# Combine, norm and the attention's first norm in one stage, the state-space kernel's products beside the last experts, and no load stage

## The chip, the core and the metric

The kernel is one program for one core of a Trainium2 chip. The core has TensorE (matrix products, "PE"; its weight loads are "PEld"), VectorE ("DVE"), ScalarE ("ACT"), GpSimd ("POOL") and SyncE ("SP", which here only issues DMAs), 128-partition on-chip memory (SBUF), accumulators for products (PSUM, eight banks) and DMA queues. Each engine runs its own instruction list and meets the others at semaphores. The metric is the device time of one execution in microseconds, from the first to the last instruction and what lies around them.

## What is computed

Two decoder layers on 8 x 256 = 2048 tokens of width 256, all in float32 here. After each sub-layer f the state is x = layernorm(x + f(x)). The sub-layers in order: a state-space scan ("mamba"), cross attention, a mixture of 16 experts, a linear attention block ("performer"), a cross-attention with a state-space convolution, and a retrieval layer ("peer"). What the change touches, cut from the reference:

```
# mixture of experts: each token goes to its best expert, at most C = 160 tokens per expert
dispatch = einsum('tec,td->ecd', sec_mask, tokens)
h = relu(einsum('ecd,edh->ech', dispatch, w1)); expert_out = einsum('ech,ehd->ecd', h, w2)
ans = einsum('tec,ecd->td', combine_weights, expert_out)
# then x = layernorm(x + ans); and the performer starts with a norm of that
x1 = layer_norm(x, ln1_scale, ln1_bias)          # eps 1e-6
q, k, v = x1 @ wq, x1 @ wk, x1 @ wv
# state-space kernel of the later convolution: depends on weights alone
K = 2.0 * einsum('dn,dnl->dl', dC, powers).real;  Kf = rfft(K, n=2*L)
```

The kernel K has 256 taps for each of 256 channels. With tap = 16 h + l, it is, per channel d, a product of a table UU (128 x 16, over h) and a table VV (128 x 16, over l). The transform Kf is a product with a constant matrix ("dft_kernel").

## The kernel before

**Tiling.** The state X lies in SBUF as 16 tiles (NT) of 128 tokens x 256; XT is the same state transposed (2 blocks of 128 features x 2048 tokens). Norms work in groups of four tiles (GT). Every stage is a `Stage` with its own buffers, semaphores and a block: engines start it together and leave it together. Between the six big stages all semaphores are cleared and all engines meet (L2716 and around).

**Start.** `stage_load` (L135) asks for XT and ident and waits for both. `stage_mamba` (L514) then asks for W, WO and small weights on SP, in that order; TensorE waits for W (`w_loaded`) and makes, for each group of 512 tokens and each of four channel blocks, a product UP and a gate product ZP (L601). ScalarE (L609, L623) and VectorE (L633, L649 to 656) first wait for seven small loads (`loaded`). SP then loads X itself (2 MB) and, once TensorE's second products allow, stores rows (L572).

**Experts.** `moe_route` scatters the tokens to a buffer in DRAM; `moe_experts` (L1481) runs over 16 experts (numbered 0 to 15): TensorE turns the tokens, makes HP = tokens x W1 (L1560), later turns the last expert's answers back (L1543) and makes YT (L1573), which ScalarE copies (L1593); VectorE and ScalarE apply the relu (L1617, L1589); VectorE copies answers to YE (L1608) and SP stores them in DRAM (L1509). Beside this, GpSimd and ScalarE compute the tables UU and VV (`S4dTables`, L1117; the last step is L1253).

**Combine.** In a stage of its own, `norm_only` (L388) runs with `Combine` (L1256) beside it. TensorE makes 256 products of 16 x 16 outputs (L1299, one per channel); VectorE copies them eight times (L1315), each copy 512 columns wide on 16 partitions; SP moves the result within SBUF in 16 DMAs (L1292); TensorE transforms it (L1309) and VectorE copies it to KF (L1321). GpSimd gathers each token's answer from DRAM in 16 indirect DMAs (L1278). VectorE, behind its eight copies, adds the weighted answers (L1285) and norms X in place (L442 statistics, L445, L450 reciprocal, L408), one tile in four on GpSimd.

**Performer.** `stage_performer` (L1692) starts with a second `norm_only` (name pfln) that reads X, writes X1, and whose transposes (L480) ScalarE scales into XT (L501). Then a block in which GpSimd sets a buffer to one (L1722), and `products` (L166), the projections: 48 jobs on TensorE (L204) through a ring of eight banks, copied by VectorE alone (L1639, L1644, L1731).

What sets the order of work is this program order on each engine, and SP's and GpSimd's DMA queues, which take transfers in the order they are issued.

## Time and profile before

| | us |
|---|---|
| median of 3 timed runs | 2629.9 (2623.7 to 2634.0) |
| the profiled execution | 2615.5 |
| its span, first to last instruction | 2613.7 |
| TensorE busy in it | 2245.9 (86%) |
| VectorE busy | 1705.5 (65%) |
| ScalarE busy | 961.5 (37%) |
| GpSimd busy | 852.7 (33%) |

The profile is one execution; its times are to be compared with each other, and the span with the profiled execution's own time. Busy shares are means over stages with different limits, so a stretch is read in the timeline: each row gives start, duration, engine, line of the source, output and inputs by name, how many instructions were merged, and in brackets the engine's idle time ahead of it with what ended it.
### The profile page before, as it was taken

To read this page: it belongs to the slowest core of one execution; us is meant where nothing else is said; L and a number is where in the kernel's file an instruction comes from. 1 tells how busy PE (TensorE), PEld (TensorE's weight loads), DVE (VectorE), ACT (ScalarE), POOL (GpSimd) and SP (SyncE) were. 2 spreads that over 40 slices of the span, in tenths; PEclk is the share of its full clock that TensorE was granted. 3 is DMA by queue.
4 is the path that set the end of the run, shared out by engine and by line. 5 is a ranking of instruction groups with operands and counts; after the bars stand their busy time and mean duration, and the time that the engine had idled before them with its cause. 6 is when DMAs were issued, how large, how long until landed. Compare 5 with 4: busy or idle time off the path is not lost. (4 is left out here: it accounts for less than half of the span.)

```text
span 2613.7 us, 34978 instructions
## 1 busy us (share of the span) xinstructions
PE 2245.9 (86%) x12808; PEld 1537.1 (59%) x12808; DVE 1705.5 (65%) x4406; ACT 961.5 (37%) x1900; POOL 852.7 (33%) x471
## 2 busy tenths in 40 slices
PE   7788888998964994998995787879699889999997
PEld 2355555634654993465563444336466678888886
DVE  5799999515653126464147996541488788888886
ACT  2398898315846212055312432032123322222220
POOL 0198888004508954052011332431200111111110
PEclk9899999999987996999997888989799899999999
DMA  3121111000023662101000000020300000000001
GB/s 97 38 81 49 49 51 39 11 0 1 1 104 125 224 226 75 35 2 40 0 21 19 1 1 1 1 79 1 129 1 1 3 1 1 1 1 1 1 1 33
DMA packets 57902, 101.02 MB, mean 39 GB/s; under 512 B 7874, under 2 KB 39490, under 8 KB 56452
## 3 DMA queue, kind: packets, MB, share of 16 engines
q1 hardware_dynamic: 56196, 94.59, 10.8%
q0 software_dynamic: 1536, 4.20, 0.5%
q8 instruction: 102, 1.67, 0.3%
q14 instruction: 68, 0.56, 0.1%
HBM read 88.94 MB, written 9.57 MB: 38 GB/s over the span
## 5 line engine op out<-in xcount | busy, mean ns | idle before, releaser
L749 POOL TENSOR_TENSOR XT<-mamba_DU,scan_BS 128x1024 f32<-128x1024 f32 x128 | 299.1, 2361 | 156.3 <-DMA scan_BS<-mamba_rows 118.5
L878 DVE TENSOR_TENSOR_SCAN scan_H<-scan_AB,XT 128x512 f32<-128x512 f32 x256 | 296.2, 1208 | 8.5 <-POOL XT L749 5.0
L2488 PE MATMUL ex_HP<-XT,pe_DOWN 128*128 128x256 f32 x1024 | 246.5, 387 | 7.1 <-PEq L2334 6.3
L2519 PE MATMUL ex_OP<-pe_UP,ex_GH 128*128 128x256 f32 x1024 | 231.5, 380 | 0.0
L2549 ACT ACTIVATE ex_GH<-ex_HP 128x512 f32<-128x512 f32 x128 | 76.5, 599 | 379.3 <-PE ex_HP L2488 344.6
L763 PEld LDWEIGHTS scan_TP<-ident,scan_H 128*128 128x128 f32 x1024 | 120.1, 142 | 157.9 <-DVE scan_H L878 81.3
L808 ACT ACTIVATE scan_AB<-mamba_E,mamba_AA 128x510 f32<-128x510 f32 x256 | 198.7, 776 | 38.4 <-DVE scan_H L878 34.1
L2488 PEld LDWEIGHTS ex_HP<-XT,pe_DOWN 128*128 128x128 f32 x1024 | 192.0, 192 | 31.9 <-issue 6.4
L2519 PEld LDWEIGHTS ex_OP<-pe_UP,ex_GH 128*128 128x128 f32 x1024 | 194.0, 190 | 26.0
L772 PE MATMUL scan_YT<-mamba_BC,ident 128*128 128x512 f32 x384 | 198.5, 599 | 4.1 <-ACT scan_YS L824 2.3
L763 PE MATMUL scan_TP<-ident,scan_H 128*128 128x128 f32 x1024 | 147.6, 278 | 46.5 <-DVE scan_H L878 46.5
L2575 POOL TENSOR_TENSOR ex_AS<-ex_AS,pe_IV 128x512 f16<-128x512 f16 x32 | 52.9, 1683 | 361.9 <-DVE ex_AS L2623 361.9
L2600 DVE TENSOR_TENSOR ex_L<-ex_IOTA,ex_KEYS 128x4096 f16<-128x4096 f16 x64 | 151.8, 2372 | 2.2
L817 ACT ACTIVATE mamba_BC<-scan_TP,scan_CT 128x512 f32<-128x512 f32 x192 | 129.6, 675 | 3.9 <-PE scan_TP L763 3.9
L2346 PE MATMUL sides_QP<-XT,sides_WQ 128*128 128x512 f32 x256 | 118.1, 616 | 5.2 <-ACT sides_QN L2371 3.0
L2674 DVE SCALAR_TENSOR_TENSOR ex_GH<-ex_GP,ex_GH 128x1024 f32<-128x1024 f32 x64 | 78.4, 1224 | 61.1 <-issue 32.5
L1617 DVE TENSOR_SCALAR experts_HT<-experts_HP 128x320 f32<-128x320 f32 x32 | 15.7, 492 | 132.6 <-PE experts_HP L1560 132.6
L2036 PE MATMUL tk_TP<-tk_DG,tk_PP 128*128 128x128 f32 x256 | 55.2, 403 | 47.3 <-ACT tk_DG L2129 47.3
L2508 PEld LDWEIGHTS ex_GP<-ex_R,ex_L 128*128 128x128 f16 x2048 | 77.8, 117 | 17.3 <-DVE ex_L L2600 5.2
L2346 PEld LDWEIGHTS sides_QP<-XT,sides_WQ 128*128 128x128 f32 x256 | 49.0, 197 | 62.8 <-issue 55.8
L2508 PE MATMUL ex_GP<-ex_R,ex_L 128*128 128x32 f16 x2048 | 77.6, 191 | 9.2 <-issue 4.7
L2036 PEld LDWEIGHTS tk_TP<-tk_DG,tk_PP 128*128 128x128 f32 x256 | 52.0, 311 | 54.9 <-ACT tk_DG L2129 54.9
(417 smaller groups left out, 4639.5 us busy)
## 6 DMA issues: line engine op xcount, KB each, us to landing
moe_W<-in_L_ffn_w SPq DMA_DIRECT2D x32, 1024.0 KB, 7.5
scan_BS<-mamba_rows SPq DMA_DIRECT2D x64, 256.0 KB, 3.1
pe_DOWN<-in_L_ffn_down SPq DMA_DIRECT2D x1, 4096.0 KB, 13.4
pe_UP<-in_L_ffn_up SPq DMA_DIRECT2D x1, 4096.0 KB, 22.8
moe_dispatch<-s4t_BOTH SPq DMA_DIRECT2D x1, 2560.0 KB, 8.7
experts_XE<-moe_dispatch SPq DMA_DIRECT2D x16, 160.0 KB, 2.4
moe_answers<-experts_YE SPq DMA_DIRECT2D x16, 160.0 KB, 3.2
XT<-in_xT SPq DMA_DIRECT2D x1, 2048.0 KB, 7.4
```

The lines of the kernel that those rows point to most:

```text
L749: pool.tensor_tensor(BU[:, r % 2, cs], tokens(DU, cs, r // DS), row, ALU.mult).then_inc(bu_ready, 1)
L763: ins = pe.transpose(TP[:, i % SLOTS, c * P:(c + 1) * P], H[:, r % 2, c, tb * P:(tb + 1) * P], ident[:, 0:P])
L772: pe.matmul(YT[:, tb, :], ident[:, 0:P], HT[:, n % 4, :], start=(s == 0), stop=(s == DS - 1)).then_inc(y_added, 1)
L808: act.activation(later(AB[:, n % 2, :]), later(tokens(E, c, g)), ACT.Exp, scale=AA[:, 2 * c, s:s + 1], bias=AA[:, 2 * c, s:s + 1]).then_in ...
L817: act.activation(HT[:, n % 4, :], TP[:, item(r, tb) % SLOTS, :], ACT.Copy, scale=CT[:, TB * g + tb, s:s + 1]).then_inc(act_read, 1)
L878: v.tensor_tensor_scan(H[:, r % 2, c], AB[:, n % 2, :], BU[:, r % 2, c], 0.0, ALU.mult, ALU.add).then_inc(h_ready, 1)
L2036: ins = pe.matmul(TP[:, n % 2, 0, k * P:(k + 1) * P], PP[:, n % 2, h, k * P:(k + 1) * P], DG[:, h, :], start=(h == 0), stop=(h == XH - 1))
L2346: ins = pe.matmul(QP[:, g, :], WQ[:, k, c * P:(c + 1) * P], XT[:, k, g * G4:(g + 1) * G4], start=(k == 0), stop=(k == KD - 1))
L2488: ins = pe.matmul(HP[:, n % 2, a, :], DOWN[:, k, 2 * q + a, :], XT[:, k, b * BLK:(b + 1) * BLK], start=(k == 0), stop=(k == KD - 1))
L2508: ins = pe.matmul(GP[:, n % 2, t, :], L[:, n % 2, t // RUN, :, t % RUN], R[:, n % 2, t // RUN, :, t % RUN], start=True, stop=True)
L2519: ins = pe.matmul(OP[:, m % 2, 0:D], GH[:, b % 2, j, a * P:(a + 1) * P], UP[:, j, :], start=(j == 0), stop=(j == J2 - 1))
L2600: v.tensor_tensor(L[:, n % 2], numbers(P), along(0, P), ALU.is_equal).then_inc(left_ready, 1)
```

## The change

- `stage_load` is no longer run ahead of `stage_mamba`. There, SP issues W, the first 512-token group of XT, ident (in WO's place among the seven small loads), the small weights, the other three groups of XT, WO, X. TensorE waits for each group of XT, SP for WO.
- The state-space kernel's products move into `moe_experts`, in two chunks of 64 products, in experts 14 and 15 ahead of their YT products. One product takes two channels (32 x 32 outputs, of which the two 16 x 16 blocks on the diagonal are used) and goes to one of four 32-partition strips. VectorE copies a chunk at once (128 x 512) into KA, which reuses a table's buffer; SP stores the used blocks to a DRAM tensor in 2 x 8 DMAs, ahead of the last answers' store. The results YT lose their second PSUM buffer to the chunk.
- The stage with `Combine` and `norm_only` goes. `combine_norms`, the performer's first stage, gathers, adds, takes one set of statistics per tile, and from it gets both norms: X1 is normalised twice in one step on VectorE, X by ScalarE (128 x 256, scale and bias per token). GpSimd only gathers.
- The projections get four jobs more, at their end: the transform, with the kernel and its matrix loaded by SP during `combine_norms`.

The diff, cut (allocations of semaphores and small buffers, and the removed class `Combine`, whose code is that of the kernel before):

```diff
--- before.py
+++ after.py
...
+
+
+def first_group(io, XT, g):
+    tok = slice(g * G4, (g + 1) * G4)
+    return XT[:, :, tok], io["xT"].rearrange("(k p) t -> p k t", p=P)[:, :, tok]
...
                     @block.sync
                     def _(sp):
                         sp.dma_start(W[:], io["L0_attn_in_projT"].rearrange("(k p) n -> p k n", p=P)).then_inc(w_loaded, 16)
-                        sp.dma_start(WO[:], io["L0_attn_out_projT"].rearrange("(k p) n -> p k n", p=P)).then_inc(loaded, 16)
+                        sp.dma_start(*first_group(io, XT, 0)).then_inc(xt_loaded[0], 16)
+                        sp.dma_start(ident[:], io["ident"]).then_inc(loaded, 16)
...
+                        for g in range(1, NG):
+                            sp.dma_start(*first_group(io, XT, g)).then_inc(xt_loaded[g], 16)
+                        sp.dma_start(WO[:], io["L0_attn_out_projT"].rearrange("(k p) n -> p k n", p=P)).then_inc(wo_loaded, 16)
                         x_load.issue(sp)
                         x_load.wait(sp)
+                        sp.wait_ge(wo_loaded, 16)
...
                         for g in range(NG):
+                            pe.wait_ge(xt_loaded[g], 16)
...
-        pool.tensor_tensor(self.UU[:], self.UU[:], self.U2[:], ALU.add)
...
+        pool.tensor_tensor(self.UU[:], self.UU[:], self.U2[:], ALU.add).then_inc(self.factors_ready, 1)
...
+def moe_experts(nc, io, ident, dispatch, answers, kernel, tables, W1, W2, first_loads):
+    TILES = 4
+    PAIR = 2
+    KN = P // TILES
+    KI = KN // PAIR
+    CHUNKS = D // P
+    FIRST_CHUNK = NE - CHUNKS
     with Stage(nc, "experts") as st:
+        KA = tables.TT[:].rearrange("p d l -> p (d l)")[:, 0:CHUNKS * PAIR * LO * KI].rearrange("p (n a l i) -> p n a l i", n=CHUNKS, a=PAIR, l=LO)
         XE = st.sb("XE", [HC_, 2, 2, D])
...
-        YT = st.ps("YT", [P, 2, 512])
+        YT = st.ps("YT", [P, 512])
+        KP = st.ps("KP", [P, 512])
...
                 store(NE - 2)
+                for n in range(CHUNKS):
+                    sp.wait_ge(kernel_copied, n + 1)
+                    for j in range(TILES):
+                        for a in range(PAIR):
+                            r, d = j * KN + a * HI, n * P + j * KN + a * KI
+                            sp.dma_start(kernel[:, :, d:d + KI].rearrange("l h d -> h l d"), KA[r:r + HI, n, a]).then_inc(kernel_stored, 16)
                 store(NE - 1)
                 for i in range(2):
                     sp.wait_ge(stored[i], 16 * (NE // 2))
+                sp.wait_ge(kernel_stored, 16 * TILES * PAIR * CHUNKS)
 
...
+                def kernel_products(n):
+                    pe.wait_ge(tables.factors_ready, 1)
+                    if n:
+                        pe.wait_ge(kernel_copied, n)
+                    for i in range(KI):
+                        for j in range(TILES):
+                            d = slice(n * P + j * KN + i * PAIR, n * P + j * KN + (i + 1) * PAIR)
+                            ins = pe.matmul(KP[j * KN:(j + 1) * KN, i * PAIR * LO:(i + 1) * PAIR * LO], tables.UU[:, d, :].rearrange("p a h -> p (a h)"),
+                                            tables.VV[:, d, :].rearrange("p a l -> p (a l)"), start=True, stop=True)
+                    ins.then_inc(kernel_ready, 1)
...
                     if e:
                         turn_back(e - 1)
+                    if e >= FIRST_CHUNK:
+                        kernel_products(e - FIRST_CHUNK)
                     pe.wait_ge(relu_act, 2 * (e + 1))
                     pe.wait_ge(relu_dve, 2 * (e + 1))
-                    if e >= 2:
-                        pe.wait_ge(ys_copied, e - 1)
+                    if e:
+                        pe.wait_ge(ys_copied, e)
...
+                def kernel_out(n):
+                    v.wait_ge(kernel_ready, n + 1)
+                    v.tensor_scalar(KA[:, n].rearrange("p a l i -> p i a l"), KP[:].rearrange("p (i a l) -> p i a l", a=PAIR, l=LO), 2.0, None, ALU.mult).then_inc(kernel_copied, 1)
...
+def combine_norms(nc, name, X, X1, XT, ident, GA, rest, scale, bias, loads, ahead):
+    NG = NT // GT
+    with Stage(nc, name) as st:
+        TP = st.ps("TP", [P, 4, 512])
+        with st.block() as block:
+            @block.gpsimd
+            def _(pool):
+                for t in range(NT):
+                    pool.indirect_dma_start(out=GA[:, t, :], out_offset=None, in_=rest.answers,
+                                            in_offset=bass.IndirectOffsetOnAxis(ap=rest.FROM[:, t:t + 1], axis=0)).then_inc(gathered[t // GT], 16)
+            @block.sync
+            def _(sp):
+                loads.issue(sp)
+                for a in ahead:
+                    a.issue(sp)
+            @block.vector
+            def _(v):
+                ch = Chain(v, dve_chain)
+                for g in range(NG + 1):
+                    if g < NG:
+                        tiles = slice(g * GT, (g + 1) * GT)
+                        v.wait_ge(gathered[g], 16 * GT)
+                        for t in range(g * GT, (g + 1) * GT):
+                            ins = v.scalar_tensor_tensor(X[:, t, :], GA[:, t, :], rest.WT[:, t:t + 1], X[:, t, :], ALU.mult, ALU.add)
+                        ch.link(ins)
+                        for t in range(g * GT, (g + 1) * GT):
+                            ins = v.bn_stats(raw[:, t, :], X[:, t, :])
+                        ch.link(ins)
+                        for t in range(g * GT, (g + 1) * GT):
+                            ins = v.bn_aggr(MV[:, t, :], raw[:, t, :])
+                        ch.link(ins)
+                        v.tensor_scalar(RS[:, 0, tiles], MV[:, tiles, 1], 1.0, 1e-5, ALU.mult, ALU.add)
+                        v.tensor_scalar(RS[:, 1, tiles], MV[:, tiles, 1], 1.0 + 1e-6, 1e-11, ALU.mult, ALU.add).then_inc(var_ready, 1)
+                    if g:
+                        tiles = slice((g - 1) * GT, g * GT)
+                        v.wait_ge(std_ready, g)
+                        v.reciprocal(RS[:, :, tiles], RS[:, :, tiles]).then_inc(scale_ready, 1)
+                        v.wait_ge(scale_ready, g)
+                        for t in range((g - 1) * GT, g * GT):
+                            v.tensor_scalar(X1[:, t, :], X[:, t, :], MV[:, t, 0:1], RS[:, 1, t:t + 1], ALU.subtract, ALU.mult).then_inc(normed, 1)
+                        v.scalar_tensor_tensor(NB[:, tiles], MV[:, tiles, 0], -1.0, RS[:, 0, tiles], ALU.mult, ALU.mult).then_inc(bias_ready, 1)
+            @block.tensor
+            def _(pe):
+                for t in range(NT):
+                    pe.wait_ge(normed, t + 1)
+                    if t >= 4:
+                        pe.wait_ge(turned_read, t - 3)
+                    for k in range(KD):
+                        ins = pe.transpose(TP[:, t % 4, k * P:(k + 1) * P], X1[:, t, k * P:(k + 1) * P], ident[:, 0:P])
+                    ins.then_inc(turned, 1)
+            @block.scalar
+            def _(act):
+                loads.wait(act)
+                for g in range(NG + 1):
+                    if g < NG:
+                        tiles = slice(g * GT, (g + 1) * GT)
+                        act.wait_ge(var_ready, g + 1)
+                        act.activation(RS[:, :, tiles], RS[:, :, tiles], ACT.Sqrt).then_inc(std_ready, 1)
+                    if g:
+                        for t in range((g - 1) * GT, g * GT):
+                            act.wait_ge(turned, t + 1)
+                            for k in range(KD):
+                                ins = act.activation(XT[:, k, t * P:(t + 1) * P], TP[:, t % 4, k * P:(k + 1) * P], ACT.Identity,
+                                                     scale=scale[:, k:k + 1], bias=bias[:, k:k + 1])
+                            ins.then_inc(turned_read, 1)
+                        act.wait_ge(bias_ready, g)
+                        for t in range((g - 1) * GT, g * GT):
+                            act.activation(X[:, t, :], X[:, t, :], ACT.Identity, scale=RS[:, 0, t:t + 1], bias=NB[:, t:t + 1])
...
+            WK_ = s1.sb("WK_", [P, LO // LB, NF, P])
+            KB = s1.sb("KB", [P, LO // LB, D])
...
+                     (MASK[:], io["causal"]), (KEPS[:], io["L1_attn_key_eps"]), (WK_[:], io["dft_kernel"])] +
+                     [(KB[l * HI:(l + 1) * HI], inputs.kernel[l::LB].rearrange("i h d -> h i d")) for l in range(LB)])
+            GA = QT[:].rearrange("p c t -> p (c t)")[:, 0:NT * D].rearrange("p (t d) -> p t d", d=D)
+            combine_norms(nc, "pfln1", X, X1, XT, ident, GA, inputs, scale=LN[:, 0, :], bias=LN[:, 1, :],
+                          loads=Loads(nc, "pfln1", [(LN[:], io["L1_attn_ln"])]), ahead=[loads])
+            inputs.free()
...
+            def by_channel(v, out, product):
+                return v.tensor_copy(out.rearrange("p (m i a) -> p m a i", i=LO, a=2), product.rearrange("p (m a i) -> p m a i", i=LO, a=2))
+
+            for q in range(NF):
+                jobs.append((KF[:, q, :], [(WK_[:, i, q, :], KB[:, i, :]) for i in range(LO // LB)], by_channel))
             products(nc, "pfproj", jobs, loads, dve_only=True, ahead=[mlp_loads], evictor_needs=[loads])
...
-        stage_load(nc, io, X, XT, ident, with_x=stage_mamba not in stages)
+        if stage_mamba not in stages:
+            stage_load(nc, io, X, XT, ident, with_x=True)
...
```

## Rows read from the trace of the kernel before

**Rows 1.** Timeline from 0 to 25 us: start, us, engine, line, form [idle before].

```profile
0.73 0.43 SPq L99 DMA_DIRECT2D XT<-in_xT  x1
...
9.28 0.38 SPq L559 DMA_DIRECT2D mamba_in_W<-in_L_attn_in_projT  x1
9.71 0.46 SPq L560 DMA_DIRECT2D mamba_WO<-in_L_attn_out_projT  x1
...
14.37 3.78 PE L601 MATMUL mamba_in_UP<-XT,mamba_in_W 128*128 128x512 f32 x4 [14.37 <-DMA mamba_in_W<-in_L_attn_in_projT]
...
18.64 0.31 ACT L609 ACTIVATE mamba_AA<-mamba_AA 128x128 f32<-128x128 f32 x1 [8.08 <-DMA mamba_AA<-in_L_attn_A_log]
...
20.95 0.60 ACT L623 ACTIVATE mamba_in_SIL<-mamba_in_ZP 128x512 f32<-128x512 f32 x1 [0.70 <-PE mamba_in_ZP L601]
```

**Rows 2.** DMA issues of the page: KB each, us from issue to landing.

```profile
mamba_WO<-in_L_attn_out_projT SPq DMA_DIRECT2D x1, 512.0 KB, 6.2
```

**Rows 3.** Timeline from 970 to 986 us: the last expert and the next stage.

```profile
973.91 0.49 DVE L1617 TENSOR_SCALAR experts_HT<-experts_HP 128x320 f32<-128x320 f32 x1 [5.91 <-PE experts_HP L1560]
...
976.68 4.58 PE L1573 MATMUL experts_YT<-experts_HT,moe_W 128*128 128x160 f32 x32 [0.20 <-issue]
...
982.46 0.69 DVE L1608 COPY experts_YE<-experts_YP 80x512 f32<-80x512 f32 x1 [5.25 <-PE experts_YP L1543]
985.60 0.36 SPq L99 DMA_DIRECT2D combine_WK<-in_dft_kernel  x1
```

**Rows 4.** Timeline of GpSimd from 945 to 965 us: the last table step.

```profile
950.92 8.88 POOL L1253 TENSOR_TENSOR s_UU<-s_UU,s4t_U 128x4096 f32<-128x4096 f32 x1
```

**Rows 5.** Timeline from 985 to 1024 us; then the tile GA (ns min/median/max).

```profile
991.02 3.35 PE L1299 MATMUL combine_KP<-s_VV,s_UU 128*16 128x16 f32 x128 [0.76 <-issue]
...
991.76 1.02 DVE L1315 TENSOR_SCALAR combine_KA<-combine_KP 16x512 f32<-16x512 f32 x1 [1.52 <-PE combine_KP L1299]
...
1006.35 1.06 POOL L1278 DMA_INDIRECT s_GA<-moe_answers,moe_FROM  x1 [0.30 <-issue]
...
1010.48 1.66 DVE L1285 SCALAR_TENSOR_TENSOR X<-s_GA,moe_WT,X 128x256 f32<-128x256 f32 x4
...
1014.09 1.22 DVE L408 TENSOR_SCALAR X<-X,moenorm_MV,moenorm_RS 128x256 f32<-128x256 f32 x3
...
1015.23 1.66 DVE L1285 SCALAR_TENSOR_TENSOR X<-s_GA,moe_WT,X 128x256 f32<-128x256 f32 x4
...
1021.33 1.40 DVE L1321 COPY KF<-combine_KP 128x256 f32<-128x256 f32 x4
...
L1278 POOL DMA_INDIRECT s_GA<-moe_answers,moe_FROM x16: 942/947/2108, 986.3 to 1006.4; - x16
...
DMA to landing us min/median/max: 2.7/3.0/4.0
```

**Rows 6.** DMA from 15.5 to 17 us; the output stores of the page.

```profile
DMA packets 2199, 0.27 MB, mean 177 GB/s; under 512 B 1927, under 2 KB 2199, under 8 KB 2199
...
out<-X SPq DMA_DIRECT2D x4, 512.0 KB, 2.9
```

**Rows 7.** Timeline from 1024 us; window 1045 to 1051 (busy, PEclk, DMA).

```profile
1024.38 0.37 SPq L99 DMA_DIRECT2D pf_LN<-in_L_attn_ln  x1
...
1035.59 5.78 ACT L501 ACTIVATE XT<-pfln_TP,pf_LN 128x128 f32<-128x128 f32 x16
...
1045.48 9.82 PE L204 MATMUL pfproj_ring<-XT,pg_WQ 128*128 128x512 f32 x16 [6.10 <-PEq L1719]
...
1045.00:1051.00 6.00, 5.52 (x7) 2.45 (x8) 0.69 (x1) 0.00 (x0) 0.15 (x1) 0.50 0.67 234
```

**Rows 8.** Grouped lines (busy us, mean ns, idle before); then one row of the timeline.

```profile
L1403 PE MATMUL route_LT<-XT,route_GW 128*32 128x512 f32 x16 | 3.6, 1061 | 4.7 <-DMA route_TI<-in_spill_rows 4.7
...
L1034 ACT ACTIVATE attn_PR<-attn_SC,attn_MX 128x256 f32<-128x256 f32 x128 | 58.8, 479 | 7.6 <-DVE attn_MX L1074 7.6
...
1103.20 13.98 PE L204 MATMUL pfproj_ring<-pg_WV,XT 128*128 128x256 f32 x64
```

More of the change, by code:

```diff
@@ L467, in _ @@
             def _(pe):
-                if beside:
-                    beside.kernel_products(pe)
-                    beside.transform(pe)
                 if XT is not None:
@@ L1335, in stage_moe @@
                                                   for W, n in ((W1, "L0_ffn_w1"), (W2, "L0_ffn_w2"))])
[L1336 to L1343 removed]
+        tables = S4dTables(st, st, io)
+        moe_route(nc, io, X, XT, ident, TO, rest.FROM, rest.WT, dispatch, first_loads, tables)
+        moe_experts(nc, io, ident, dispatch, rest.answers, rest.kernel, tables, W1, W2, first_loads)
+    return rest
 def moe_route(nc, io, X, XT, ident, TO, FROM, WT, dispatch, first_loads, tables):
```

114 lines of the change are left out of this document (32 added, 82 removed).

## The prediction, made before the changed kernel was run

> **What bounds the kernel now.** The program is a row of stages with a barrier after each, so the time is a sum over stages, and each touched stretch has its own limit. I read in this order: the timeline of the first 25 us, the experts' end, the stretch from the experts to the projections, then single tiles, DMA counts and grouped lines for prices.
>
> Start. XT (2 MB) and ident are loaded in a stage of their own; the weight W is asked for only at 9.28, and TensorE's first product runs at 14.37. The first gate product is whole 6.6 us later (20.95), and ScalarE and VectorE's loop, which sets the pace from there on, starts with it [rows 1].
>
> Experts. TensorE is the chain: 32 records of W2 products in 4.58 us, as many of W1 before them, and only 0.20 us idle, while VectorE waits 5.9 us for it [rows 3]. GpSimd's last table step ends at 950.92 + 8.88 = 959.8 [rows 4].
>
> Then 59.9 us (985.60 to 1045.48 [rows 3, 7]) hold three things in a row: the state-space kernel (256 small products, 8 copies, 16 moves, a transform) with the gathers in its shadow; the combine and the first norm; after a boundary, the attention's norm.
>
> **Part by part.** The profiled run took 2615.5 us (span 2613.7); the median of the timed runs is 2629.9, 14.4 above. I sum against the profiled run and shift by those 14.4.
>
> *A, the load stage goes.* W is now issued first (0.73, where XT was), then group 0 of XT (512 KB). The trace has this pair in size: W and WO, 1 MB and 512 KB in succession. WO landed at 9.71 + 6.2 = 15.9, 6.6 after W's issue [rows 1, 2]. So TensorE starts at 0.73 + 6.6 = 7.3, not 14.37: -7.0. Bounds: as late after W's issue as now (5.1) gives -8.5; as late as the old load stage ended (9.28) gives -5.1. Seven small loads must land before ScalarE's first step; it now ran 9.4 after W's issue (18.64), and there is one DMA more ahead of it: 10.6. ScalarE is ready for the gate 1.6 later (20.95 less its idle of 0.70, less 18.64 [rows 1]), 12.2; the gate product comes at 7.3 + 6.6 = 13.9. Hidden by 1.7 us. XT's groups 1 to 3, WO and x follow on SP: group 1 is needed only after four products of group 0, WO stages later, and the row stores behind SP's new wait for WO come after TensorE's first projections. Nothing.
>
> *B, the products in experts 14 and 15.* 256 products become 128, 64 in each of two chunks, two channels in one (32 by 32), written to four column strips. A product is two matmul records, so a chunk has 128 of them. 128 records of the 16-column form take 3.35 us, with the idle before them 4.1 [rows 5]. I take 3.6 a chunk and subtract the 0.2 idle: +7.0 on the chain; nothing on TensorE hides them. The other end: for the gate's logits four strips ran side by side, 16 records of 512 columns in 3.6 us, 0.23 each [rows 8], where lone ones take 0.94 (four in 3.78 [rows 1]). If that held for 32 columns a chunk would be 0.9 and the term +1.6. I take the dear end: 16 columns take 26 ns and 160 take 143 [rows 3], so the small ones are not paced by their columns, and strips need not help.
>
> The Trainium skill speaks on both sides. TensorEngine Tiling (Array Packing), Instruction Overhead: some 60 cycles per matmul however few its columns, an estimate of 25 ns; the 26 ns row agrees. TensorE: Matmul & The Clock Gate, Part 3, The mechanism: strips start about 4 ns apart. The second is a rival below.
>
> Waits and queues. The tables are ready 7 us before the first chunk. The results' PSUM buffer is single now, but the turn ahead already awaited its copy. VectorE's copy (16x512 took 1.02 us [rows 5]; for 128 partitions 0.7 to 1.1) falls in its idle of 5.9. On SP, 16 stores go in ahead of the last answers store, each of 256 runs of 64 B. Issues cost 0.38 to 0.46 in [rows 1]; for the finer ones I take 0.5: chunk 0 goes out from 981.3 to 985.3, chunk 1 to 989.3, and the last answers are copied at 983.15 + 7.0 = 990.2 [rows 3]. The last expert covers them with 0.9 to spare; that is gone at 0.55 each, and at 0.8 they cost 3 us. The data: reads of this grain ran at 2199 packets in 1.5 us on 16 engines, 11 ns each per engine [rows 6]; 4096 runs are then 3 us, hidden. No row has small runs written to DRAM. Lower bound 0; upper the output's store, 512 rows of 1 KB, 32 per engine, landing in 2.9 [rows 6]: 90 ns each, 256 per engine 23 us, which ends at 1004 instead of 992. I take +0.8, nearest to the reads. B together +7.8, from +1.6 to +20.
>
> *C, boundaries.* The boundary with the semaphores' clearing (1022.73 to 1024.38, 1.65 us [rows 5, 7]) moves to where a plain one stood, about 0.4: +1.25. The new stage starts at S = 985.6 + 7.8 + 1.25 = 994.7.
>
> *D, one stage for combine and both norms.* Gathers: first at S + 0.7, each 0.95 + 0.30, 3.0 to land [rows 5], so groups of four are there at S + 7.6, 12.6, 17.6, 22.6. VectorE per group: answers and statistics, 1010.48 to 1014.09 less a reciprocal of 0.18, plus two small steps, 3.75; later reciprocal, four normalisings (three took 1.14) and bias, 0.2 + 1.55 + 0.12 = 1.87 [rows 5]. With 0.2 lost to the 2.5 MB of loads that SP issues beside: group 1 from 12.8 to 16.55, then 0 to 18.4, group 2 to 22.15, 1 to 24.0, group 3 to 27.8, 2 to 29.65, 3 to 31.5. So from group 1 VectorE is the limit and the gathers have 1 us to spare. ScalarE: eight 128x128 at 0.37 a group, 2.95 (16 took 5.78 [rows 7]), and now four 128x256 with two pointers. No row shows these: 0.37 (half the columns) to 0.60; I take 0.45, near the exponential of this size at 0.48 [rows 8]. The tail is ScalarE's: group 2 from 29.1 to 32.1 and 33.9, group 3 to 36.9 and 38.7; I take S + 38.5. GpSimd's share of the normalising falls away; its cover is VectorE's 0.4 a group, counted above. The memset's block stays: 1041.37 to 1045.48, 4.1 [rows 7]. Projections start at S + 42.6, so C and D are 1.25 + 42.6 - 59.9 = -16.0; from -18 (gathers early, 0.37 on ScalarE) to -4 (every gather as slow as the one of 2.11). TensorE's clock is 0.50 at the projections' start [rows 7], and after a stretch with still less work on it it will be the same.
>
> *E, four transform jobs at the projections' end.* Each is four records of 128x256, as a value job: 64 such in 13.98 us [rows 8], 0.87 a job: +3.5. VectorE keeps up with a copy each; the tile's loads are long in place.
>
> Sum: -7.0 + 7.8 - 16.0 + 3.5 = -11.7. 2615.5 becomes 2603.8; by the median 2618.
>
> **Rivals.**
> *Forecast*, 3.5 us either way: 2614.5 to 2621.5.
> *Gathers exposed.* One of sixteen took 2.11 us [rows 5]. Should SP's loads do that to the first eight, the last lands 9.3 later; VectorE's lead takes part, and the stage ends some 5 us later: 2623; with all sixteen, 2630. Against: the last one took 1.06 beside the same VectorE work.
> *Strips side by side.* At 0.9 us a chunk the chain gains 5.4, but SP's stores then set the end, at about +4.5: 2614 to 2615. For it the logits row, against it the 26 ns. This is the second page's rule.
> *The small stores decide, slower than before.* Sixteen stores in one queue, the last answers and the stage's end behind them. They start at 981.3 and are free up to 990; each us more is one on the end, and the whole gain is gone when they take 20.5 us, 1.3 per store or 80 ns per run and engine. At 95 ns the result is 2633; one after another at a read's full landing of 3 us, 48 us and 2657. For it: no row has such writes. Against: 11 ns for such reads.
> *The load stage gives less*: -4 instead of -7 if a late small load holds ScalarE: 2621.
>
> **How the numbers follow.** Forecast 0.58, strips 0.16, gathers 0.12, small stores 0.08, load 0.06. The bound of 0.5% is 13.1 us (2616.8), about what a measurement of this kernel can tell from no change; the forecast lies on its edge, a third of it below. Faster 0.19 + 0.16 = 0.35; slower needs 2643, the far part of the stores and a little beside, 0.05; the rest, 0.60, is within. The range for 8 in 10 goes from strips with a cheap tail (2609) to exposed gathers (2629).
>
> **What would show it.** First product at 7.3. Experts 14 and 15 longer by 3.6 us each; the last answers store issued right behind VectorE's copy, the stage over some 2.4 us later. In the new stage VectorE without idle from group 1 on, ScalarE last. From the last W2 product's end to the projections 49 us, 64.2 now. Four jobs more, 3.5 us. Against it: SP still issuing when the last answers are copied, a store landing long after its issue, VectorE waiting for gathers, a chunk of 1 or 2 us. Only the price of 64-byte writes could make it wrong by far.

## The result, and the profile after

| us | before | after |
|---|---|---|
| median of 4 timed runs | 2632.0 (2623.7 to 2635.7) | 2598.4 (2593.4 to 2601.4) |
| the profiled execution | 2615.5 | 2596.8 |
| its span | 2613.7 | 2595.0 |

The ratio is 0.988, with a 95% interval of 0.987 to 0.990: some 31 us less by the ratio and 33.6 by the two medians, where 12 were forecast. 2598.4 lies below the range, which began at 2609. (The ratio and the medians differ by 2 to 3 us in several runs below; gains in us are differences of medians where nothing else is said.) The two profiled executions differ by only 18.7. That these numbers disagree is the key to the case.

The rows of after that answer to those of before come first. The timeline of its start and of its last two experts (start, us, engine, line, form, in brackets the idle before; answers to [rows 1, 3]):

```profile
7.72 3.75 PE L601 MATMUL mamba_in_UP<-XT,mamba_in_W 128*128 128x512 f32 x4 [7.72 <-DMA XT<-in_xT]
...
10.43 0.31 ACT L609 ACTIVATE mamba_AA<-mamba_AA 128x128 f32<-128x128 f32 x1 [8.41 <-DMA mamba_AA<-in_L_attn_A_log]
...
959.76 1.30 PE L1512 MATMUL experts_KP<-moe_VV,moe_UU 128*32 128x32 f32 x128
...
961.09 1.03 DVE L1584 TENSOR_SCALAR moe_TT<-experts_KP 128x512 f32<-128x512 f32 x1 [0.47 <-PE experts_KP L1512]
...
971.57 9.31 SPq L1478 DMA_DIRECT2D s_kernel<-moe_TT  x16
...
977.41 0.69 DVE L1580 COPY experts_YE<-experts_YP 80x512 f32<-80x512 f32 x1 [4.67 <-PE experts_YP L1502]
980.93 0.45 SPq L1461 DMA_DIRECT2D moe_answers<-experts_YE  x1
984.36 0.36 SPq L99 DMA_DIRECT2D pf_LN<-in_L_attn_ln  x1
```

The 16 small stores by themselves (line L1478; ns of one, min/median/max):

```profile
L1478 SPq DMA_DIRECT2D s_kernel<-moe_TT x16: 447/450/1924, 971.6 to 980.4; - x16
```

The reader is to see three things. A chunk of products takes 1.30 us. The 16 small stores hold SyncE's queue for 9.31 us: 0.45 for the issue of one, 0.49 from one to the next, except for one of them, the second, which takes 1.92. So the last answers, copied at 977.41 + 0.69 = 978.10, are sent out only at 980.93, 2.8 late.

The timeline of the new combining stage, from its start at 984.36 to the projections (answers to [rows 5, 7]):

```profile
985.07 1.06 POOL L1699 DMA_INDIRECT pg_QT<-moe_answers,rest_FROM  x1 [33.22 <-POOLq L2800]
...
988.58 4.62 SPq L99 DMA_DIRECT2D pg_KB<-s_kernel  x8
988.95 0.95 POOL L1699 DMA_INDIRECT pg_QT<-moe_answers,rest_FROM  x1 [0.30 <-issue]
...
996.66 1.67 DVE L1716 SCALAR_TENSOR_TENSOR X<-pg_QT,rest_WT,X 128x256 f32<-128x256 f32 x4 [18.56 <-DMA pg_QT<-moe_answers,rest_FROM]
...
1021.27 2.91 ACT L1757 ACTIVATE XT<-pfln_TP,pf_LN 128x128 f32<-128x128 f32 x8
1024.01 2.12 ACT L1762 ACTIVATE X<-X,pfln_NB,pfln_RS 128x256 f32<-128x256 f32 x4
1026.38 3.51 POOL L1800 MEMSET pg_VA<- 128x4096 f32 x1 [21.37 <-ACTq L1797]
...
1030.23 4.61 PE L204 MATMUL pfproj_ring<-XT,pg_WQ 128*128 128x512 f32 x5 [9.97 <-PEq L1797]
```

The issue of the fourth gather runs from 988.95 to 989.90, and its group is first worked on at 996.66, 7.7 after that issue began and 12.3 after the stage's start. ScalarE ends the stage at 1026.13, 41.8 after it.

### The profile page after: what moved, and what is told of

Same layout as the page of the kernel before. It is cut to its first block and busy times, and to the rows that moved or that the text cites. A ratio compares the mean times of both kernels' runs of the same rounds, so it can differ in the third digit from the quotient of the medians.

```text
span 2595.0 us, 34415 instructions
## 1 busy us (share of the span) xinstructions
PE 2226.3 (86%) x12552; PEld 1522.9 (59%) x12552; DVE 1689.6 (65%) x4368; ACT 967.7 (37%) x1912; POOL 839.9 (32%) x463
## 5 line engine op out<-in xcount | busy, mean ns | idle before, releaser
L2119 PE MATMUL tk_TP<-tk_DG,tk_PP 128*128 128x128 f32 x256 | 48.8, 368 | 48.4 <-ACT tk_DG L2212 48.4
L1545 PE MATMUL experts_YT<-experts_HT,moe_W 128*128 128x160 f32 x512 | 76.9, 310 | 7.2 <-ACT experts_HT L1561 6.8
```

## The experiments

Two theories at the start. The first: the change's own steps are worth 30 us, and I mis-sized them. The rival: the profile of before shows an execution that isn't like the timed ones.

**The two kernels again, and the change in two halves.** `e3` has the new load order alone (part A); `e4` all the rest (B to E).

> The kernel before, unchanged, run as if it were a variant: it tells how far two profiles and two sets of timed runs of one kernel lie apart. The sum over the touched stretches gives -11.7 us, the two profiled spans differ by 18.7, the timed medians by 33. Theory 'clock': the part beyond the stretches is TensorE's granted clock at the starts of later, untouched stages, which falls out differently from run to run; then this profile's span differs from 2613.7 by 5 to 20 us, at the starts of stages, and the ratio to before is 1.000 within 0.3%. Theory 'change': the extra belongs to the change; then this span is again within 3 us of 2613.7.

> The changed kernel again, on the chip of the other runs of this call. Theory 'clock' (the extra is chance): ratio nearer to 0.9955 (-11.7 us) than to 0.988. Theory 'change' (the extra is carried by one of its parts): ratio 0.988 again, -30 us.

> Only the load stage is removed, as in the change; all else as before. The sum gives -6.6 us at the first product and -6.2 at the scan: ratio 0.9976. If this part carries the extra 19 us of the timed runs, ratio 0.990 to 0.991.

> The changed kernel with the old load stage back. The sum over its stretches gives -8.6 up to the projections' start and +3.5 for the transform's jobs, -5.2 at the attention's core: ratio 0.998. If this part carries the extra, ratio 0.990 to 0.991.

Beside a kernel before at 2631.2 (23 runs): e1 2626.1 (ratio 0.998, 0.997 to 0.9995), e2 2600.1 (0.988, 0.986 to 0.990), e3 2625.3 (0.998, 0.997 to 0.999), e4 2606.7 (0.991, 0.990 to 0.993). But e1 is the kernel before itself, and it lies 5 us below the other runs of the same kernel: differences of that size mean nothing here. e3 is only 0.8 below e1, so the medians don't show what A is worth; its trace does, the scan starts at 114.7 and in e1 at 121.4. e4 is 19 us below e1 where the sum had 5, so the surplus is in B to E. The profile of e1 took 2629.0 and not 2615.5, 13.5 more. One place alone holds more than that: from the experts' first product to the attention's norm it has 228.0 us, 210.3 in the profile that I had, which is 17.7 more; the other stages together are some 4 us shorter. So neither theory of e1 had it right: the profile of before is not like the others, and not by the clock at the start of later stages. The TensorE timeline of that place, in e1:

```profile
985.33 1.83 PE L1299 MATMUL combine_KP<-s_VV,s_UU 128*16 128x16 f32 x64 [3.22 <-PEq L1504]
987.33 0.32 PE L1299 MATMUL combine_KP<-s_VV,s_UU 128*16 128x16 f32 x6 [0.17 <-issue]
988.09 0.34 PE L1299 MATMUL combine_KP<-s_VV,s_UU 128*16 128x16 f32 x6 [0.43 <-issue]
988.84 0.29 PE L1299 MATMUL combine_KP<-s_VV,s_UU 128*16 128x16 f32 x4 [0.42 <-issue]
```

and two windows of it (busy us and records of PE, PEld, DVE, ACT, POOL, then PEclk, DMA share, GB/s):

```profile
985.30:1008.80 23.50, 6.84 (x122) 4.55 (x122) 1.00 (x1) 1.28 (x1) 15.26 (x16) 0.51 0.39 112
1008.80:1019.10 10.30, 10.22 (x391) 10.11 (x391) 6.16 (x7) 0.00 (x0) 0.00 (x0) 0.78 0.02 5
```

In the first 23.5 us TensorE gets through 122 of the 512 records (two to a product), 64 at a stretch and then 58 in bursts, waiting for nothing that the profile shows ("issue"). These are the microseconds in which GpSimd has its 16 gathers on the way (x16 under POOL). The issue of the last gather runs from 1004.88 to 1005.83. With the 3.0 from issue to landing of [rows 5] it lands near 1007.9, and from 1008.80 on TensorE runs 391 records with hardly a gap. In the profile of before the block of 128 in [rows 5] took 3.35 us, and the whole row of 512 took 16. e3 shows the bursts as well.

**Are the gathers the cause?** e5 is the kernel before, with GpSimd waiting for the last product:

```diff
     def gather(self, pool):
+        pool.wait_ge(self.k_ready, D // self.DB)
         for t in range(NT):
```

> The kernel before, with one edit: GpSimd issues its 16 gathers of the experts' answers only after TensorE has done the state-space kernel products of that stage, not beside them. Theory (beside the gathers TensorE is fed its small matmuls in bursts of 1 to 6 every 0.7 us): the 512 products run without gaps in about 16 us, 985.3 to about 1001; the first gathers land some 5 us after that, and the additions are at work near 1010 where the kernel before has them near 1020; 8 to 11 us shorter than the kernel before, ratio 0.996 to 0.997. Rival (the products run in bursts by themselves, whatever GpSimd does): they still take 23 us, the gathers come behind them, and the kernel is 7 to 8 us longer, ratio 1.003.

```profile
987.33 4.61 PE L1300 MATMUL combine_KP<-s_VV,s_UU 128*16 128x16 f32 x170 [3.24 <-PEq L1505]
...
992.58 9.21 PE L1300 MATMUL combine_KP<-s_VV,s_UU 128*16 128x16 f32 x342 [0.64 <-issue]
```

The timeline of e5, TensorE: 512 records in 14.5 us. The statistics behind the first additions start at 1010.5, in e1 at 1021.6. VectorE then waits for later gathers (from there to the attention's norm it takes 25.2 us and took 20.6), so that the stage is 8.4 us shorter than in e1, at the low end of the forecast. The whole took 2623.9, ratio 0.998 (0.997 to 0.999) to a kernel before at 2628.6: 4.7 us less, no more than e1 shows for no change at all. Products by themselves don't come in bursts. That it is the gathers beside them is not shown yet, for e5 ran on another chip than e1.

The next step held the gathers only until half of the products are done (`D // self.DB // 2`), as e12 and again as e16; e11 and e18 issue plain copies of the same size in place of the indirect gathers, so that the sums are of other rows (arguments left out, `...`):

```diff
-            pool.indirect_dma_start(out=self.GA[:, t, :], out_offset=None, in_=self.answers, in_offset=...)
+            pool.dma_start(self.GA[:, t, :], self.answers[t * P:(t + 1) * P])
```

> The kernel before, with GpSimd's gathers issued after half of the 512 products are done. Theory (TensorE is short of instructions only while gathers are being issued): the first 256 products run unbroken in about 8 us, to 993.5; then bursts of 1 to 6 until the last gather has landed, near 1016, and the rest at 26 ns each; the last product is done at 1017 to 1021. Rival (only the start of a stage is short of instructions, before its code has been fetched once): the last 256 run unbroken too, and the last product is done at 1001.

> The kernel before, with each of GpSimd's 16 indirect gathers of the stage replaced by a plain copy of 128 consecutive rows, same bytes, same queue; this leaves out the choice of rows by the routing, so the sums are of other rows. Theory A (it is the indirect form, its descriptors made from indices, that keeps TensorE short of instructions): the products run unbroken, 16 us for 512, and the additions start at 1005 to 1010 instead of 1020: 10 to 15 us shorter than the kernel before. Theory B (any transfers that GpSimd issues there do it): bursts as before, additions at 1020, no difference beyond the shorter issue.

Neither showed bursts: e12 2615.4 (one run), e11 2611.9 (ratio 0.999, 0.9985 to 1.0004). But the kernel before took 2614.1 beside them (2607.8 to 2616.8, 15 runs), 10 to 17 us less than elsewhere. The records number the chips: these runs were on chip 11, those told of so far on 12 and 15. On chip 11 e12, with the gathers issued from 991.02 on, beside the second half of the products, ran like this:

```profile
983.17 4.61 PE L1300 MATMUL combine_KP<-s_VV,s_UU 128*16 128x16 f32 x170 [3.24 <-PEq L1505]
988.43 3.35 PE L1300 MATMUL combine_KP<-s_VV,s_UU 128*16 128x16 f32 x128 [0.65 <-issue]
992.16 3.35 PE L1300 MATMUL combine_KP<-s_VV,s_UU 128*16 128x16 f32 x128 [0.38 <-issue]
995.89 2.30 PE L1300 MATMUL combine_KP<-s_VV,s_UU 128*16 128x16 f32 x86 [0.38 <-issue]
```

So my theory was incomplete: in some places the gathers starve TensorE and in another they don't. The same kernel, as e16, went to chip 12, with both kernels beside it.

> The kernel before once more, for one more execution of its combining stage. The chip that is drawn decides: where its runs lie at 2624 to 2635 us the 512 kernel products come in bursts of 1 to 6 and the additions start near 1021; where they lie at 2608 to 2617 us the products run in about 17 us in blocks of 128 and the additions start near 1004.

> The kernel before with GpSimd's gathers issued after half of the products, once more. Theory (TensorE is short of instructions only on the chips where the kernel before takes 2624 us and more, and only while gathers are issued): on such a chip the first 256 products run in about 8 us and the rest in bursts until the last gather has landed, near 1014, last product 1014 to 1020; on the other kind of chip all 512 run in 17 us. Rival (only the start of a stage is short of instructions): no bursts on either.

> The kernel after once more, to see what the change is worth on the chip that is drawn. Theory (17.7 us of the gain is the short supply of instructions, which the kernel after does not meet anywhere): on a chip where the kernel before takes 2608 to 2617 us, the kernel after takes 2596 to 2603, 12 to 18 us less, ratio 0.993 to 0.995; where it takes 2624 to 2635, 30 us less, ratio 0.988. Rival (the kernel after is faster by its own work alone): 30 us less on either.

e16 on chip 12, TensorE and GpSimd:

```profile
989.77 3.35 PE L1300 MATMUL combine_KP<-s_VV,s_UU 128*16 128x16 f32 x128 [0.66 <-issue]
993.50 0.63 PE L1300 MATMUL combine_KP<-s_VV,s_UU 128*16 128x16 f32 x19 [0.38 <-issue]
994.38 0.31 PE L1300 MATMUL combine_KP<-s_VV,s_UU 128*16 128x16 f32 x6 [0.25 <-issue]
...
1013.58 0.19 PE L1300 MATMUL combine_KP<-s_VV,s_UU 128*16 128x16 f32 x1 [1.16 <-issue]
1014.98 3.97 PE L1300 MATMUL combine_KP<-s_VV,s_UU 128*16 128x16 f32 x143 [1.21 <-issue]
...
992.36 1.06 POOL L1279 DMA_INDIRECT s_GA<-moe_answers,moe_FROM  x1 [33.41 <-PE combine_KP L1300]
...
1011.23 0.94 POOL L1279 DMA_INDIRECT s_GA<-moe_answers,moe_FROM  x1 [0.30 <-issue]
```

TensorE ran without long gaps until 994.1, 1.8 us after the first gather's issue began, and again from 1014.98, 2.8 us after the last one's issue ended (1012.17). On this chip, then, the bursts follow the gathers when these are moved. e13 repeats e1: 64 records, then bursts, then 391 from 1007.58. Chip 12 showed the bursts on two occasions, and chip 11, between them, did not; chip 11 was seen only once, so "chip" may stand for something else of that hour. The kernel before took 2624.3 on chip 12 this time and e14 2600.8, ratio 0.990 (0.987 to 0.993); I had said 30 us and 0.988, and 24 were measured, though the runs of before there spread from 2621.9 to 2635.1.

**What of the gathers does it?** e18 (plain copies, again on GpSimd's queue) and e19 (the same copies issued by SyncE ahead of WK).

> The kernel before with plain copies of 128 consecutive rows in place of GpSimd's 16 indirect gathers, once more; the sums are of other rows. It tells something only where the kernel before lies at 2622 us and more. Theory A (the indirect form does it): no bursts, 512 products in 17 us, 10 to 18 us shorter than the kernel before. Theory B (any transfer that GpSimd issues does it): bursts until the last copy has landed, near 997, since 16 issues take 8.6 us there and not 20; products done near 1007, 10 to 12 us shorter.

> The kernel before with the same 16 plain copies issued by SyncE, ahead of its load of WK, and none by GpSimd; the sums are of other rows. Theory (transfers of GpSimd's own queue keep TensorE short of instructions): the 512 products run in blocks of 128 in 17 us on every chip, additions start near 1004, 15 to 18 us shorter than the kernel before where that lies at 2622 us and more. Rival (busy DMA engines do it, whoever fills them): bursts as long as the copies run, some 8 us at 2.1 MB, products done near 1008.

Both were on chip 8, the kernel before at 2626.0 (2624.2 to 2635.2). e18:

```profile
985.77 4.70 PE L1298 MATMUL combine_KP<-s_VV,s_UU 128*16 128x16 f32 x170 [3.24 <-PEq L1503]
991.03 3.35 PE L1298 MATMUL combine_KP<-s_VV,s_UU 128*16 128x16 f32 x128 [0.57 <-issue]
...
986.21 8.62 POOL L1278 DMA_DIRECT2D s_GA<-moe_answers  x16 [25.97 <-POOLq L1503]
...
q0 software_dynamic: 768, 2.10, 27.0%
```

The last row is the DMA of 985.7 to 1009.7: the same 768 packets and 2.10 MB in GpSimd's queue, but no bursts. From the experts' first product to the attention's norm e18 has 210.2 us, as the first profile of before (210.3). It took 2613.2, ratio 0.994 (0.992 to 0.996), 13 us less. e19 has none either: 2607.2, ratio 0.992 (0.990 to 0.994). This speaks for the indirect form, against the bytes and the queue, but does not prove it. There is no trace of the kernel before on chip 8; that it has the bursts there is read from its time alone. And the copies are issued in 8.6 us, the gathers in 20, so the pace changed with the form.

**The sizes within the new kernel.** Three single edits of the kernel after, on chip 15, where the kernel after itself was not run; so they are compared by the stages in their traces, and their medians tell little. e6 turns the loops of the products, so that neighbours stand on the same strip; e7 holds SyncE's loads until the last group is gathered; e8 sends chunk 0's stores before expert 14's answers.

```diff
# e6, kernel_products
-                    for i in range(KI):
-                        for j in range(TILES):
+                    for j in range(TILES):
+                        for i in range(KI):
# e7, combine_norms, SyncE, ahead of the loads for the next stage
+                sp.wait_ge(gathered[NG - 1], 16 * GT)
# e8, SyncE, chunk by chunk
+                store_kernel(0)     # ahead of the store of expert 14's answers
-                for n in range(CHUNKS):
+                for n in range(1, CHUNKS):
+                    store_kernel(n)
```

> The kernel after, with the order of the loops in the kernel products turned: all products of one strip of 32 columns of TensorE stand together, before those of the next strip, where the kernel after alternates between strips from one product to the next. Theory (neighbouring products overlap only because they lie on different strips): a chunk of 128 products takes about 3.4 us (26 ns each) instead of 1.30 us, and the two chunks add some 4 us, of which part lies on the path: 0 to 4 us longer. Rival (10 ns for each is what any order gives): chunk 1.3 us, no difference.

```profile
960.90 3.94 PE L1512 MATMUL experts_KP<-moe_VV,moe_UU 128*32 128x32 f32 x128
```

e6: 3.94 us a chunk instead of 1.30, and the next stage starts 3.4 later (987.78); 2604.7. Alternating between the strips is what makes the products cheap.

> The kernel after, with SyncE's loads of the next stage's weights held back in the combining stage until the last group's answers are gathered. Theory (2.5 MB of loads share the DMA engines with the gathers, so that the first group is answered 12.3 us after the stage starts instead of 7.6): the first group is answered at 7.6 to 8 us, the stage is some 4.5 us shorter, and the whole is 4 to 4.5 us shorter than the kernel after unless the loads then come late for the projections, where up to 3 us may be given back. Rival (the gathers are slow by their own number and queue): first group at 12 us as before, and the kernel is 0 to 5 us longer for the late loads.

```profile
984.17 0.36 SPq L99 DMA_DIRECT2D pf_LN<-in_L_attn_ln  x1
991.58 1.67 DVE L1717 SCALAR_TENSOR_TENSOR X<-pg_QT,rest_WT,X 128x256 f32<-128x256 f32 x4 [13.06 <-DMA pg_QT<-moe_answers,rest_FROM]
...
1027.37 5.20 PE L204 MATMUL pfproj_ring<-XT,pg_WQ 128*128 128x512 f32 x7 [9.98 <-PEq L1798]
```

e7: the first group is there 7.4 after the stage's start and not 12.3, so the loads had delayed the gathers. Only 2.7 of these 4.9 us reach the stage's end (43.2 after its start, in the kernel after 45.9): with the first group early, VectorE waits 1.6 for the second, whose gathers are issued 1.25 us apart. 2593.8.

> The kernel after, with the 8 stores of the first chunk of kernel products put ahead of expert 14's answers store in SyncE's queue, and those of the second ahead of expert 15's. Theory (the last answers store is issued 2.8 us after its data stand, because SyncE still issues 16 stores of 0.58 us): with 8 of them gone from before it the last store is issued within 0.3 us of its data, and the combining stage starts 2 to 3 us earlier; whole 2 to 3 us shorter than the kernel after. Rival (the store of expert 14 or the weights' loads behind the first chunk become late and take it back): no difference within 1 us.

```profile
977.93 0.30 SPq L1461 DMA_DIRECT2D moe_answers<-experts_YE  x1
981.21 0.36 SPq L99 DMA_DIRECT2D pf_LN<-in_L_attn_ln  x1
```

e8: the last answers leave 0.03 after their copy ends (977.21 + 0.69), and the stage starts 3.15 earlier than in the kernel after. The whole took 2597.6.

**A version that beats both.** e9 puts the memset behind the gathers; e10 joins e7, e8, e9 and gives the last two groups' normalising of X to VectorE; e17 is e10 with the ones written by VectorE at the stage's start.

```diff
# e9, GpSimd, behind its 16 gathers
+                pool.memset(VA[:].rearrange("p t h d -> p (t h) d")[:, :, LD:2 * LD], 1.0)
# e17, VectorE, before its first wait, in its place
+                v.memset(VA[:].rearrange("p t h d -> p (t h) d")[:, :, LD:2 * LD], 1.0)
# e10 and e17, VectorE, at the end
+                for t in range(ON_ACT * GT, NT):
+                    v.tensor_scalar(X[:, t, :], X[:, t, :], MV[:, t, 0:1], RS[:, 0, t:t + 1], ALU.subtract, ALU.mult)
```

> The kernel after, with GpSimd's memset of VA put behind its gathers in the combining stage, and its own block removed. Theory (the block between the stages, 3.51 us of memset and its two boundaries, is on the path; beside the gathers' end GpSimd is idle): projections start 3.9 to 4.2 us earlier after the stage's start, whole 4 us shorter than the kernel after. Rival (GpSimd's memset of 4096 elements per partition slows VectorE at the port that they share): VectorE's operations of the last groups get longer and 1 to 3 us are given back.

```profile
1004.82 5.37 DVE L1733 TENSOR_SCALAR pf_X<-X,pfln_MV,pfln_RS 128x256 f32<-128x256 f32 x4
...
1005.87 3.53 POOL L1701 MEMSET pg_VA<- 128x4096 f32 x1
```

e9's stage lasts 45.4, against 45.9: nothing of the 4.1 is won. The four normalisings take 5.37 us where they took 1.39, since VectorE gets no further with them while GpSimd's memset runs. The rival had it, at a larger price than I gave it. The Trainium skill says so (SBUF — State Buffer, SBUF: two separate sides): VectorE and GpSimd share a pair of ports, and a GpSimd operation that holds it shuts out, for its whole length, a VectorE operation that needs the pair, which not all do. The trace agrees, 4.0 us for a memset of 3.53. In e10, with the same memset, both kinds can be seen:

```profile
1002.31 3.53 POOL L1706 MEMSET pg_VA<- 128x4096 f32 x1
...
1002.51 0.38 DVE L1729 BATCH_NORM_AGGREGATE pfln_MV<-pfln_raw 128x2 f32<-128x6 f32 x4
...
1002.92 2.95 DVE L1731 TENSOR_SCALAR pfln_RS<-pfln_MV 128x4 f32<-128x4 f32 x1
```

The aggregations run through at their usual 0.38, in the midst of the memset. The first TENSOR_SCALAR, 0.17 elsewhere, ends with the memset.

> The kernel after, with four edits together: loads held until the last gather, the first chunk's stores ahead of expert 14's answers, the memset behind the gathers, and ScalarE's normalisation of X for the last two groups given to VectorE at its end. By the single runs: loads -2.6 to -4, stores -3.1, memset -4.1, X on VectorE -1 to -3.7 (ScalarE's 8 operations of 0.52 us leave its end of the stage, VectorE gets 8 of 0.41 us behind the last transposition's input). Sum -11 to -15 us against the kernel after, so about 2585 us, ratio to the kernel before 0.983 to 0.985. Rival (the parts share one path: with the loads held they land after the projections' start, and TensorE waits for WQ): half of it, 2592 us.

> The kernel with the four edits together, but VA's ones are written by VectorE at the start of the combining stage, where it waits for the first gather in any case, and not by GpSimd behind its gathers, where its 3.53 us held up VectorE's operations. Theory (VectorE and GpSimd shut each other out, so that the memset had only changed its place): 2.5 to 3.5 us shorter than the four edits with the memset on GpSimd, about 2584 us, projections start at 1015 to 1016. Rival (VectorE's memset shuts GpSimd out while it writes the descriptors of the first gathers, as the Trainium skill's page SBUF tells of operations in a mode with two ports): the first gathers come 2 to 4 us late, and nothing is won.

```profile
982.05 1.06 POOL L1704 DMA_INDIRECT pg_QT<-moe_answers,rest_FROM  x1 [30.38 <-POOLq L2808]
982.27 3.47 DVE L1716 MEMSET pg_VA<- 128x4096 f32 x1 [4.25 <-PEq L2808]
983.42 0.95 POOL L1704 DMA_INDIRECT pg_QT<-moe_answers,rest_FROM  x1 [0.30 <-issue]
...
988.69 1.67 DVE L1723 SCALAR_TENSOR_TENSOR X<-pg_QT,rest_WT,X 128x256 f32<-128x256 f32 x4 [2.95 <-DMA pg_QT<-moe_answers,rest_FROM]
...
1017.16 4.61 PE L204 MATMUL pfproj_ring<-XT,pg_WQ 128*128 128x512 f32 x5 [2.29 <-PEq L1700]
```

e10 took 2586.9 on chip 11, 0.990 (0.989 to 0.992) of the kernel before there, and e17 2586.9 on chip 12, 0.985 (0.981 to 0.988), 14 us less than the kernel after on the same chip. The stage lasts 37.3 in e10 (981.14 to 1018.45) and 35.8 in e17 (981.34 to 1017.16), so moving the ones to VectorE is worth 1.5 and not 2.5 to 3.5; as medians the two are of different chips and tell nothing of it. VectorE's memset did not delay the gathers beside it: they are issued at the same pace, and the first group is there 7.35 after the start as in e7.

## Why the prediction was wrong

**The step that failed: "I sum against the profiled run and shift by those 14.4."** The sum itself held on the profile that it was made on. By it the projections were to start 15.2 us earlier and the attention's core 11.7 earlier; in the profile of after they start 15.25 (1030.23 for 1045.48 [rows 7]) and 11.8 earlier (1106.2 for 1118.0). That it held to 0.1 is luck: the parts below came out 2.1 us worse than forecast when added up (0.8 and 3.3 worse, 2.05 better), and the stages from the scan to the experts, which the change doesn't touch, happened to be 2.1 shorter in the profile of after (690.6 for 692.7; 692.3 in e2).

The shift assumed that whatever made the timed runs longer than the profiled one would still be there after the change. It was not spread over the program: the bursts beside the gathers cost 17.7 us, in the one stretch that the change takes apart. In the prediction's terms, the 59.9 from the stage's start to the projections, which C and D replace, are 77.9 in e1 (985.29 to 1063.2). The new kernel does its small products where no gather is on the way, and so never meets the bursts. 11.7 + 17.7 = 29.4; on chip 12 31 (26 against e1) and 24 were measured. Without the shift the sum said 2603.8. The last line of the prediction, that only the price of 64-byte writes could make it wrong by far, did not see this at all.

It could have been suspected. The profiled execution (2615.5) lay 8 us below the lowest of the three timed runs, which lay within 11 us of each other. So it was probably of another population, and the question to ask was where the 14 us sit and whether the change touches that place. That the profile of before came from a chip like number 11 fits its time and its unbroken products, but no record says so. There the kernel after itself was not run; e9, whose stage is 0.5 us shorter, was: 2597.3 for 2614.1, ratio 0.994 (0.993 to 0.996), 17 us by the medians and 15 by the ratio. That is 3 to 5 more than the sum. Between the two profiled executions 18.7 less 11.8 leaves 6.9, and it lies in stages that the change doesn't touch (transposes before the S4 stage 321.8 for 326.7, token projections 59.8 for 61.5, sides 183.7 for 185.5, experts at the end 540.8 for 539.2). Executions of the very same kernel differ by as much in these stages (326.7 and 322.0 in e2 and e14), so I put this down to chance.

**A, the load stage: -7.0 forecast.** First product at 7.72 (forecast 7.3); ScalarE's first step at 10.43 (10.6). The scan starts 6.2 earlier (6.7 between e1 and e3). Right in mechanism, 0.8 too much.

**B, products in the experts: +7.8 forecast, +6.0 measured** (from the experts' first product to the issue of the last answers' store, 175.1 for 169.1). The sum was near by two errors that cancel in part. The chunk of 128 records costs 1.30 us, not 3.6: the strips' rival was right, and the 26 ns row, of products that share one strip, could not speak for it. With 0.196 us for one record by itself, the records start (1.30 - 0.196) / 127 = 8.7 ns apart with strips alternating, and (3.94 - 0.196) / 127 = 29.5 ns apart without (e6), at a granted clock of 1.00 in both. The Trainium skill's two rules (TensorE: Matmul & The Clock Gate, Part 3, The mechanism, and TensorEngine Tiling (Array Packing), Instruction Overhead) fit these two cases; the trace agrees with the second's estimate of 25 ns roughly, and shows twice the 4 ns that the first gives for neighbours at different positions in the array. Against that gain, the last answers were 2.8 late, which e8 gave back. All 16 stores stood behind the answers of expert 14, as forecast, and cost the forecast 0.5 each. But the cheaper second chunk brought the last answers nearer by 2.3 us, as the strips' rival had it, so that the cover of 8.9 us became 6.5, and one store's issue took 1.92. "The small stores decide" was half right: their issue cost something, their data did not pile up. One was issued every 0.49 us, and each landed 1.8 after its issue (median, 3.5 at most). The prediction's own price for that queue had a slip, too: at 0.8 each the 16 stores would end 3.9 us behind the last answers, not 3.

**B and C together: +9.05 forecast, +7.0 measured** (from the experts' first product to the next stage's start, 178.5 for 171.5); C by itself is 1.0, for 1.25.

**D, the combined stage: 42.6 to the projections forecast, 45.9 measured.** Two sizes. The rival "gathers exposed" had the right cause and a wrong route: no issue became slower, but beside SP's 2.5 MB of loads VectorE could start on the first group only 7.7 us after the fourth gather's issue began, not 3.0, and the first group came at 12.3, not 7.6 (e7 shows that it is the loads). In this, "With 0.2 lost to the 2.5 MB of loads" was the wrong term. Group for group VectorE then took 5.3 us, 5.6 forecast. ScalarE's 128x256 with two pointers took 0.52, not 0.45, 0.6 us for the eight at its end. Part of the first was hidden: e7 gives back 2.7. 2.7 + 0.6 = 3.3, the difference.

**E, four more jobs: +3.5 forecast, +3.5 measured** (76.0 for 72.5).

## What to carry to other kernels

Before a profile is used as the base of a sum, its own time is to be held against the timed runs; where it lies outside of them, the difference has a place, and a change that touches that place takes it away or leaves it. A row of many tiny matmuls is better not run beside indirect gathers: on one chip here it cost next to nothing, on another 17.7 us. And work that is moved "beside" something idle is free only if the two engines don't exclude each other, and if the queue that it is put into has nothing urgent behind it.

## What the runs showed of the hardware

- Beside indirect gathers issued by GpSimd, TensorE got 1 to 6 records of small matmuls every 0.7 to 2.8 us for as long as the gathers lasted, 122 records in the first 23.5 us (e1), on chip 12 (e1, e3, e13, e16). On chip 11 the same gathers did not do it (e12), and plain copies of the same bytes through the same queue did not either on chip 8 (e18). What differs in the chips, and by which path the gathers hold the instructions back, stays open. In the first 24 us of this stage the instruction queue (q8) moved 4 packets where there were no bursts (the profile of before, e5, e12, e18), 1 where they came from the start (e1, e13) and 3 where they came in the second half (e16).
- Records of 32-column matmuls: 8.7 ns apart on alternating strips, 29.5 ns on one.
- A store of 256 runs of 64 B took SyncE 0.45 us to issue, 0.49 from one to the next; one of the 16 took 1.92 (in the kernel after; 2.09 in e2, 1.34 in e7).
- GpSimd's memset of 128x4096 held VectorE's TENSOR_SCALAR operations until its end (e9, e10), but not BATCH_NORM_AGGREGATE (e10). VectorE's own memset of that size did not slow GpSimd's gathers (e17).
